# Pieces of weights by GpSimd only behind z's normalising, and the eighth pair's bias written by ScalarE instead of added by TensorE

## The chip, the cores and the metric

One core of one Trainium2 chip. The time is device microseconds from the first to the last instruction of one execution, the median of several runs. Before the change it is 291.32 us, the median of 3 runs between 291.29 and 292.5.

## What is computed

A transformer block in float32 on 8 batches of 256 tokens with 128 features: `x + layernorm(attention(layernorm(x)))`, then `x + layernorm(ffn(layernorm(x)))`. Cut to what matters:

```python
# attention: 16 heads of 8, relative bias
qkv = x @ W_qkv + b_qkv
scores = einsum('bihd,bjhd->bhij', q, k) / sqrt(8)
rel = clip(i - j + 128, 0, 256)
scores = scores + rel_bias[rel].transpose        # (16, 256, 256), the same for each batch
out = softmax(scores) @ v, then @ W_out + b_out
# feed-forward: ternary weights, 128 -> 512 -> 512 -> 512 -> 128
h = silu((x @ w1) * s1) * ((x @ w2) * s2)
h = gelu((h @ h1) * h1s)
h = gelu((h @ h2) * h2s)
y = (h @ w3) * w3s
```

## The kernel before, in words

Each engine's program is written out by hand and they meet at semaphores alone, so the order within each engine is the order of the source.

**Attention.** The heads are taken as 8 pairs, s = 0 to 7, in each of the batches b = 0 to 7. A pair's scores (two heads, 256 x 256, 1024 columns of PSUM) are computed twice. First for the row maxima of the next batch: TensorE `max_scores` (L1236) and `max_bias` (L1244, the bias table's high part by an identity), then VectorE `maxima` (L685). The maxima are transposed (L1253), kept by ScalarE (`minus_max`, L993) and sent by DMA as an additional row of q. Then for the batch itself: the bias is put into the place first, the products `scores` (L1270) are added, ScalarE takes the exponential into a ring (`probabilities`, L1008), and TensorE forms the weighted sums of v for two pairs together (`weighted`, L1296). There are three places in PSUM for all of this; maxima and scores of a pair take turns in them (`wait_max_place`, `wait_score_place`).

The bias comes in three ways. ScalarE copies it from the table `raw` into the place (`write_bias`, L1015) for pairs 0, 1, 3, 4 and 6; VectorE does for pairs 2 and 5 (L692; 1, 2, 4, 5 and 6 in the last batch). For pair 7 (`BY_PE`) TensorE adds it behind the scores with four products by an identity, of the table's high and low parts (`score_bias`, L1281).

While batch b's scores run, batch b - 1 is finished: its heads are brought back (L1307), weighed by VectorE, transposed, projected (L1320), normalised and added to x (`attn_moments`, `residual`: y), and normalised again to z (`second_norm`, L620), which TensorE transposes (`norm_T`, L1327). A normalising needs a reciprocal root, which GpSimd computes (`inv_std`, L517). Batch b - 1's roots are waited for on GpSimd ahead of the pieces of weights.

**Pieces of weights.** GpSimd splits the 11 pieces of the feed-forward weights into high and low parts during attention (`split_weights`, L559 to L571: a cast, a subtraction, a comparison, a product), as many per batch as `SPLIT_AT` says: none, 1, 1, 2, 3, 3, 1, none. It does so right behind the roots of batch b - 1. At the start GpSimd makes the table's high parts (`table_high`, L525) and pair 7's low part (L540).

**The start.** The first two units of x (two tiles each) are normalised, transposed (`x_T`, L1169) and copied by ScalarE (L940). The first batch's rows of q and k are products of the first unit (`row_products`, L1195), less their low part (`row_lows`, L1202), which ScalarE takes and keeps in turn (L959, L967).

**Feed-forward.** Four chunks of 512 tokens, layer by layer and interleaved, each product with the high and the low part of its input (L1441, L1442). The last batch's attention is finished among them (`heads_T`, `project`), with VectorE's `layer_low` (L818) between its steps.

Of the kernel before, what the change touches and what calls it, by code (L numbers as in the profile page):

```python
# [14 lines left out]
P = 128  # L15
# [42 lines left out]
BY_PE = (7,)  # L58
BY_DVE = (2, 5)
LAST_BY_DVE = (1, 2, 4, 5, 6)  # L60
LOW_AT_SLOT = {2 * s + k: 2 * i + k for i, s in enumerate(BY_PE) for k in range(2)}
# [25 lines left out]
def build(nc, x, wq, wk, wv, bqk, brows, bv, wo, bo, ext, w1, s1, w2, s2, h1, h1s, h2, h2s, w3, w3s,  # L87
          ident_in, out):
    ctx = ExitStack()
    with ctx:  # L90
# [3 lines left out]
        def sem(name):  # L94
            return ctx.enter_context(nc.semaphore(name))
# [44 lines left out]
        rows_at = lo_at + 2 * len(BY_PE) * WIN  # L140
        room = sb("room", [P, max(rows_at + 4 * PAIRS * S, 2 * NK * CH * SLOTS)], F32R)
        table_hi = room[:, hi_at:lo_at].rearrange("p (h c) -> p h c", h=H)
        table_lo = room[:, lo_at:rows_at].rearrange("p (h c) -> p h c", h=2 * len(BY_PE))
# [97 lines left out]
        table_lo_set = sem("table_lo_set")  # L241
# [100 lines left out]
        def by_dve(b):  # L342
            return BY_DVE if b + 1 < B else LAST_BY_DVE

        def by_act(b):
            return tuple(s for s in range(PAIRS) if s not in BY_PE + by_dve(b))

# [158 lines left out]
        def _(pool):  # L506
# [13 lines left out]
            def x_inv_std(u):  # L520
                inv_std(u + 1, UNITS[u][1], UNITS[u][0])
# [10 lines left out]
            x_inv_std(1)  # L532
            x_inv_std(2)
            for s in range(PAIRS):
                table_high(s)
                if s == 5:
                    x_inv_std(3)
            for i, s in enumerate(BY_PE):
                pool.wait_ge(table_hi_pool, s + 1)
                nc.gpsimd.tensor_tensor(table_lo[:, 2 * i:2 * i + 2, :], raw[:, 2 * s:2 * s + 2, :],  # L540
                                        table_hi[:, 2 * s:2 * s + 2, :].bitcast(F32),
                                        ALU.subtract).then_inc(table_lo_set, 1)

            x_inv_std(4)
# [29 lines left out]
            for b in range(B):  # L574
                if b > 0:
                    inv_std((b - 1) * 2 + NU + 1, TPB)
                    inv_std((b - 1) * 2 + NU + 2, TPB)
                for piece in SPLIT_AT[b]:
                    split_weights(piece)
# [23 lines left out]
        def _(dve):  # L603
# [19 lines left out]
            def x_moments(u):  # L623
                first, tiles = UNITS[u]
                dve.wait_ge(x_in[u], 16)
                moments(lambda t: xs[:, first + t, :], tiles, u * 2, first)
# [34 lines left out]
            x_moments(1)  # L661
# [3 lines left out]
            spread_weights(nc.vector.tensor_copy, 0, (0,))  # L665
            dve.wait_ge(brows_in, 16)
# [6 lines left out]
            x_normalize(1)  # L673
            dve.wait_ge(ident_loaded, 16)
            nc.vector.tensor_scalar(minus_ident[:, :], ident[:, :], -1.0, None, ALU.mult).then_inc(minus_set, 1)
            dve.wait_ge(qk_w_in[2], 16)
# [184 lines left out]
            layer_low(0, 0)  # L861
            attn_moments(B - 1)
            layer_low(1, 0, (0, 1))
# [292 lines left out]
        def _(pe):  # L1156
# [49 lines left out]
            row_products(0)  # L1206
            x_T(1)
            pe.wait_ge(minus_set, 1)
            row_products(1)
            row_lows(0)  # L1210
# [46 lines left out]
            def scores(b, s):  # L1257

                if s % RPAIRS == 0:
                    pe.wait_ge(mrow_in[s // RPAIRS], (b + 1) * MROW_DMAS * 16)  # L1260
                tile = score_tile(b * PAIRS + s)
                if s in BY_PE:
                    wait_score_place(pe, b * PAIRS + s)
                elif s in by_dve(b):
                    pe.wait_ge(bias_set_dve, biases_by(by_dve, b, s))
                else:
                    pe.wait_ge(bias_set, biases_by(by_act, b, s))
                for j in range(2):
                    for half in range(2):
                        last = mm(tile[:, half, j * S:(j + 1) * S],  # L1270
                                  rows(k_rows, b, half, s)[:, j * P:(j + 1) * P], rows(q_rows, b, half, s),
                                  start=(s in BY_PE and j == 0), stop=False, skip_group_check=True)
                if s not in BY_PE:
                    last.then_inc(st_ready, 1)

            def score_bias(b, s):
                if b == 0:
                    pe.wait_ge(table_lo_set, BY_PE.index(s) + 1)
                for half in range(2):
                    for part in (table_hi[:, 2 * s + half, :], table_lo[:, LOW_AT_SLOT[2 * s + half], :]):  # L1280
                        last = mm(score_tile(b * PAIRS + s)[:, half, :], identr[:, :], windows(part, 0, P, 2, S),  # L1281
                                  start=False, stop=True, skip_group_check=True)
                last.then_inc(st_ready, 1)
# [70 lines left out]
            for b in range(B):  # L1354
                more = b + 1 < B
                for s in range(PAIRS):
                    if more or s not in BY_PE:
                        scores(b, s)
# [13 lines left out]
                    if s in BY_PE and more:  # L1372
                        score_bias(b, s)
                    if s + 1 in BY_PE and not more:

                        scores(b, s + 1)
                        score_bias(b, s + 1)
# [164 lines left out]
            def ffn(exact):  # L1542
# [20 lines left out]
                whole(layer1, 1, exact, (0, 1))  # L1563
                project(B - 1)
                whole(layer1, 1, exact, (2, 3))
# [88 lines left out]
```

## Time and profile before

| | |
|---|---|
| median of 3 runs | 291.32 us |
| the profiled execution | 292.18 us |
| its span, first to last instruction | 290.38 us |
| TensorE busy | 268.5 us (92%) |
| VectorE busy | 219.3 us (76%) |
| ScalarE busy | 205.9 us (71%) |
| GpSimd busy | 102.4 us (35%) |
| mean granted TensorE clock | 0.99 |

The span is the profiled execution's first to last instruction; the execution's own time has a little around it. Busy shares are averages over stages: attention runs to about 194 us, the feed-forward part from there to the end. A timeline row has the start in us from the span's start, the duration, the engine (PE is TensorE, DVE VectorE, ACT ScalarE, POOL GpSimd), the line, the operation, what it writes and reads, how many instructions of the kind follow each other, and in brackets how long the engine had stood idle and for whom.

### The profile page before, as it was taken

Reading aid. Unit: us, or ns where it says so; the run is one execution under the profiler, and the core shown is the slowest. Engines: PE = TensorE matmul, PEld = TensorE weight load, DVE = VectorE, ACT = ScalarE, POOL = GpSimd, SP = SyncE. Lnnn points to the kernel's source line nnn. Section 1 sums busy time; section 2 is a strip of 40 time slices with the busy share of each in tenths; the row PEclk is TensorE's granted clock in tenths of the full one; section 3 lists DMA queues with packets and bytes.
Section 4 is the critical chain, followed back from the end, with each engine's and each line's share of the span. In section 5 each row is a group of like instructions: output and inputs, shape, how many; then the busy total and the mean of one; then the engine's idle time right before and its main releaser. Section 6 shows DMA issues by size and latency. Waiting matters only on the chain.

```text
span 290.4 us, 5171 instructions
## 1 busy us (share of the span) xinstructions
PE 268.5 (92%) x1875; PEld 180.4 (62%) x1875; DVE 219.3 (76%) x442; ACT 205.9 (71%) x316; POOL 102.4 (35%) x107
## 2 busy tenths in 40 slices
PE   7999989899999999999998998899999999999980
PEld 7756645555555554565554554567887888888860
DVE  3489977889789889889889899848556843673674
ACT  2777777776786786885886876777469976896750
POOL 7616000103504305906966957018630202400111
PEclk9999999999999999999999999999999999999996
DMA  6979506232221263470320200000000000010012
GB/s 166 320 238 142 184 11 208 89 83 77 74 76 38 77 207 124 138 224 8 104 81 19 61 1 3 1 3 1 0 2 0 0 0 2 0 36 2 2 36 77
DMA packets 21356, 21.17 MB, mean 73 GB/s; under 512 B 3664, under 2 KB 18768, under 8 KB 21072
## 3 DMA queue, kind: packets, MB, share of 16 engines
q1 hardware_dynamic: 20464, 20.53, 24.8%
q8 instruction: 17, 0.28, 0.4%
q10 hardware_dynamic: 864, 0.27, 0.4%
q14 instruction: 11, 0.09, 0.1%
HBM read 14.90 MB, written 5.64 MB: 71 GB/s over the span
## 4 chain that ended last, share of the span: by engine, by line
PE 60%; DVE 22%; ACT 9%; issue 5%; DMA 1%; POOL 0%; SPq 0%; ACTq 0%; DVEq 0%
PE place L1441 10%; PE place L1442 10%; PE place L1244 8%; DVE mx L685 7%; PE pv L1296 6%; PE place L1236 4%; ACT ring L1008 4%; DVE y_and_z L620 4%; PE place L1270 4%; DVE stats L609 2%; PE place L1195 2%; DVE place L692 2%; ACT place L1015 2%; PE pv L1442 2%; PE pv L1441 2%
## 5 line engine op out<-in xcount | busy, mean ns | idle before, releaser
L685 DVE TENSOR_REDUCE mx<-place 128x4 f32<-128x1024 f32 x64 | 78.1, 1222 | 13.1 <-PE place L1244 11.8
L517 POOL TENSOR_TENSOR rstd<-mv,mhalf 128x2 f32<-128x2 f32 (+1 forms) x26 | 21.0, 809 | 153.0 <-DVE mv L617 153.0
L1008 ACT ACTIVATE ring<-place 128x1024 f32<-128x1024 f32 x64 | 65.6, 1027 | 6.3 <-PE place L1281 3.0
L1244 PE MATMUL place<-room,identr 128*128 128x512 f32 x128 | 46.9, 447 | 0.0
L1015 ACT COPY place<-raw 128x1024 f32<-128x1024 f32 x37 | 37.7, 1022 | 12.2 <-DVE mx L685 11.9
L1441 PE MATMUL place<-room,w_hi 128*128 128x512 f32 (+1 forms) x116 | 44.6, 387 | 0.7 <-DVE room L818 0.7
L1442 PE MATMUL place<-room,w_hi 128*128 128x512 f32 (+1 forms) x116 | 44.0, 382 | 0.0
L818 DVE TENSOR_TENSOR room<-ring,room 128x512 fp32r<-128x512 f32 x32 | 21.4, 690 | 18.5 <-ACT room L1096 18.5
L1296 PE MATMUL pv<-ring,vx 128*9 128x256 f32 x512 | 33.6, 380 | 0.0
L1270 PE MATMUL place<-room 33*128 33x256 f32 x256 | 31.7, 328 | 1.1 <-DVE place L692 1.0
L1236 PE MATMUL place<-room 33*128 33x256 f32 x256 | 28.3, 297 | 2.9 <-ACT ring L1008 2.7
L1270 PEld LDWEIGHTS place<-room 33*128 33x128 f32 x256 | 18.9, 184 | 15.4 <-issue 12.2
L1020 ACT COPY oT<-pv 128x256 f32<-128x256 f32 x32 | 11.8, 370 | 22.2 <-PE pv L1296 22.1
L1236 PEld LDWEIGHTS place<-room 33*128 33x128 f32 x256 | 19.8, 185 | 10.1 <-issue 6.8
L1441 PEld LDWEIGHTS place<-room,w_hi 128*128 128x128 f32 x116 | 21.8, 188 | 5.1 <-DVE room L818 0.9
L1244 PEld LDWEIGHTS place<-room,identr 128*128 128x128 f32 x128 | 19.0, 188 | 8.6
L1442 PEld LDWEIGHTS place<-room,w_hi 128*128 128x128 f32 x116 | 21.8, 188 | 4.1
L692 DVE COPY place<-raw 128x1024 f32<-128x1024 f32 x19 | 23.2, 1225 | 0.6
L1094 ACT ACTIVATE ring<-place,hs 128x512 f32<-128x512 f32 x27 | 18.5, 686 | 5.9 <-PE place L1442 5.9
L1296 PEld LDWEIGHTS pv<-ring,vx 128*9 128x9 f32 x512 | 10.9, 90 | 17.3 <-issue 9.9
L830 DVE SCALAR_TENSOR_TENSOR ring<-place,hs,raw 128x512 f32<-128x512 f32 x16 | 12.0, 750 | 12.0 <-ACT raw L1073 11.8
L1096 ACT CAST room<-ring 128x512 fp32r<-128x512 f32 x32 | 19.9, 621 | 1.0
(141 smaller groups left out, 442.9 us busy)
## 6 DMA issues: line engine op xcount, KB each, us to landing
raw<-ext SPq DMA_DIRECT2D x8, 384.0 KB, 6.9
room<-q_parts SPq DMA_DIRECT2D x48, 64.0 KB
room<-k_parts SPq DMA_DIRECT2D x48, 64.0 KB
w_lo<-h SPq DMA_DIRECT2D x2, 1024.0 KB, 5.2
q_parts<-w_hi SPq DMA_DIRECT2D x4, 256.0 KB, 3.0
k_parts<-w_hi SPq DMA_DIRECT2D x2, 512.0 KB, 3.4
xs<-x SPq DMA_DIRECT2D x3, 256.0 KB, 5.7
w_lo<-w SPq DMA_DIRECT2D x3, 256.0 KB, 2.7
```

What stands on the lines that cost most here:

```text
L517: nc.gpsimd.tensor_tensor(rstd[:, at:at + width], mv[:, at:at + width, 1], mhalf[:, 0:width], ALU.pow).then_inc(rstd_set, 1)
L685: nc.vector.tensor_reduce(mx[:, s // RPAIRS, :, :, s % RPAIRS].rearrange("p i k -> p k i"), max_tile(b * PAIRS + s)[:, :, :].rearrange("p ...
L692: nc.vector.tensor_copy(score_tile(i)[:, :, :].rearrange("p k (j n) -> p k j n", j=2), pair_windows(raw[:, :, :], i % PAIRS)).then_inc(bia ...
L818: nc.vector.tensor_tensor(lo, act_f[:, half[c], k, :], hi.bitcast(F32), ALU.subtract).then_inc((a1_lo_set, a2_lo_set)[i], 1)
L1008: nc.scalar.activation(probs[:, s % PRING, :, :, :].rearrange("p k j n -> p (k j n)"), score_tile(b * PAIRS + s)[:, :, :].rearrange("p k n ...
L1015: nc.scalar.copy(score_tile(i)[:, :, :].rearrange("p k (j n) -> p k j n", j=2), pair_windows(raw[:, :, :], i % PAIRS)).then_inc(bias_set, 1)
L1236: mm(max_tile(b * PAIRS + s)[:, half, it * S:(it + 1) * S], rows(q_rows, b, half, s)[:, it * P:(it + 1) * P], rows(k_rows, b, half, s), st ...
L1244: last = mm(max_tile(b * PAIRS + s)[:, half, :], identr[:, :], windows(table_hi[:, 2 * s + half, :], 0, P, 2, S), start=False, stop=True, ...
L1270: last = mm(tile[:, half, j * S:(j + 1) * S], rows(k_rows, b, half, s)[:, j * P:(j + 1) * P], rows(q_rows, b, half, s), start=(s in BY_PE ...
L1296: last = mm(pv[32 * r:32 * r + VC, 0:S], vx[:, b * TPB + j, 4 * g + r, :], probs[:, (2 * g + r // 2) % PRING, r % 2, j, :], start=(j == 0) ...
L1441: mm(o, w, hi, start=first, stop=False)
L1442: done = mm(o, w, lo, start=False, stop=last and exact)
```

## The change

1. `BY_PE` goes. Pair 7's bias is written by ScalarE, like that of the other pairs: `by_act` now holds 7 in each batch, `scores` waits for it like the others, `score_bias` and the low table with its GpSimd subtraction are gone. In the last batch, where pair 7's scores stand right behind pair 6's, they stay there.
2. GpSimd waits for `z_set` of the batch, behind its two roots, before it takes pieces of weights.
3. GpSimd makes tables 0 and 1 ahead of the third unit's root, and 6 and 7 behind the fourth unit's normalising (`xn_set` 4).
4. At the start VectorE normalises the first unit and spreads the q weights before the second unit's moments, and negates the identity before the second unit's normalising. TensorE takes the first two row products and the first low product before the second unit's transposes.
5. In the feed-forward part `project` of the last batch comes one output group of layer 1 later, and VectorE takes one low part before `attn_moments` and one behind it.

```diff
-BY_PE = (7,)
...
         def by_act(b):
-            return tuple(s for s in range(PAIRS) if s not in BY_PE + by_dve(b))
+            return tuple(s for s in range(PAIRS) if s not in by_dve(b))
...
             spread_weights(nc.gpsimd.tensor_copy, 1)
             x_inv_std(1)
+            table_high(0)
+            table_high(1)
             x_inv_std(2)
-            for s in range(PAIRS):
+            for s in range(2, 6):
                 table_high(s)
-                if s == 5:
-                    x_inv_std(3)
-            for i, s in enumerate(BY_PE):
-                pool.wait_ge(table_hi_pool, s + 1)
-                nc.gpsimd.tensor_tensor(table_lo[:, 2 * i:2 * i + 2, :], raw[:, 2 * s:2 * s + 2, :],
-                                        table_hi[:, 2 * s:2 * s + 2, :].bitcast(F32),
-                                        ALU.subtract).then_inc(table_lo_set, 1)
-
+            x_inv_std(3)
+
+            pool.wait_ge(xn_set, 4)
+            table_high(6)
+            table_high(7)
             x_inv_std(4)
...
                 if b > 0:
                     inv_std((b - 1) * 2 + NU + 1, TPB)
                     inv_std((b - 1) * 2 + NU + 2, TPB)
+
+                    pool.wait_ge(z_set, b)
                 for piece in SPLIT_AT[b]:
                     split_weights(piece)
...
-            x_moments(1)
             x_normalize(0)
             dve.wait_ge(row_zeros, 1)
             dve.wait_ge(bq_scaled, 1)
             spread_weights(nc.vector.tensor_copy, 0, (0,))
+            x_moments(1)
...
             layer_low(0, 0)
+            layer_low(1, 0, (0,))
             attn_moments(B - 1)
-            layer_low(1, 0, (0, 1))
+            layer_low(1, 0, (1,))
             residual(B - 1)
...
             pe.wait_ge(xT_set, 1)
             row_products(0)
+            row_products(1)
+            pe.wait_ge(minus_set, 1)
+            row_lows(0)
             x_T(1)
-            pe.wait_ge(minus_set, 1)
-            row_products(1)
-            row_lows(0)
...
-                if s in BY_PE:
-                    wait_score_place(pe, b * PAIRS + s)
-                elif s in by_dve(b):
+                if s in by_dve(b):
                     pe.wait_ge(bias_set_dve, biases_by(by_dve, b, s))
                 else:
                     pe.wait_ge(bias_set, biases_by(by_act, b, s))
...
-            def score_bias(b, s):
-                if b == 0:
-                    pe.wait_ge(table_lo_set, BY_PE.index(s) + 1)
-                for half in range(2):
-                    for part in (table_hi[:, 2 * s + half, :], table_lo[:, LOW_AT_SLOT[2 * s + half], :]):
-                        last = mm(score_tile(b * PAIRS + s)[:, half, :], identr[:, :], windows(part, 0, P, 2, S),
-                                  start=False, stop=True, skip_group_check=True)
                 last.then_inc(st_ready, 1)
...
-                whole(layer1, 1, exact, (0, 1))
+                whole(layer1, 1, exact, (0, 1, 2))
                 project(B - 1)
-                whole(layer1, 1, exact, (2, 3))
+                layer1(1, 3, exact)
```

How it moves the instructions. ScalarE's program from pair 5's exponential to the next batch's first bias, in batch b = 1; `ring<-place` are exponentials, `place<-raw` bias copies, `mrow` the maxima kept, `oT` a weighted sum kept. Before:

```order
L1008 ACTIVATE ring<-place 128x1024 [waits pv_ready,st_ready]
L993 CAST mrow<-misc 8x256 [waits mrow_in0,mT_ready]
L1008 ACTIVATE ring<-place 128x1024 [waits pv_ready,st_ready]
L1020 COPY oT<-pv 128x256 [waits pv_ready]
L940 COPY xT<-misc 128x512 [waits v_ready,xnT_ready]
L1015 COPY place<-raw 128x1024 [waits ms_read]
L1008 ACTIVATE ring<-place 128x1024 [waits pv_ready,st_ready]
```

Now:

```order
L1006 ACTIVATE ring<-place 128x1024 [waits pv_ready,st_ready]
L991 CAST mrow<-misc 8x256 [waits mrow_in0,mT_ready]
L1013 COPY place<-raw 128x1024 [waits ms_read]
L1006 ACTIVATE ring<-place 128x1024 [waits pv_ready,st_ready]
L1018 COPY oT<-pv 128x256 [waits pv_ready]
L938 COPY xT<-misc 128x512 [waits v_ready,xnT_ready]
L1013 COPY place<-raw 128x1024 [waits ms_read]
L1006 ACTIVATE ring<-place 128x1024 [waits pv_ready,st_ready]
```

The new copy, pair 7's, stands ahead of pair 6's exponential and waits for the maxima of the pair before the last.

TensorE's program at pair 7 of the same batch: scores (128x256 into a place), maxima of the next batch (128x256, then 128x512 with the identity), z's transposes. Before:

```order
L1270 MATMUL place<-room 128x256 [waits ms_read]
L1270 MATMUL place<-room 128x256 x3
L1236 MATMUL place<-room 128x256 [waits exp_done]
L1236 MATMUL place<-room 128x256 x3
L1244 MATMUL place<-room,identr 128x512 x2
L1281 MATMUL place<-room,identr 128x512 x4
L1327 MATMUL misc<-ident,y_and_z 128x128 [waits z_set,xT_set]
```

Now:

```order
L1266 MATMUL place<-room 128x256 [waits bias_set]
L1266 MATMUL place<-room 128x256 x3
L1234 MATMUL place<-room 128x256 [waits exp_done]
L1234 MATMUL place<-room 128x256 x3
L1242 MATMUL place<-room,identr 128x512 x2
L1313 MATMUL misc<-ident,y_and_z 128x128 [waits z_set,xT_set]
```

The four bias products are gone, and pair 7's scores wait for ScalarE's copy instead of the place alone.

## Rows read from the trace of the kernel before

**Rows 1.** busy time by stretches, one attention batch: PE, PEld, DVE, ACT, POOL

```profile
105.20:126.30 21.10, 20.22 (x172) 11.51 (x172) 18.76 (x33) 15.62 (x24) 10.73 (x10) 1.00 0.40 128
```

**Rows 2.** timeline of ScalarE at the joint from b = 5 to 6

```profile
152.31 1.01 ACT L1008 ACTIVATE ring<-place 128x1024 f32<-128x1024 f32 x1
...
155.90 1.02 ACT L1015 COPY place<-raw 128x1024 f32<-128x1024 f32 x1 [1.09 <-DVE mx L685]
156.85 1.02 ACT L1008 ACTIVATE ring<-place 128x1024 f32<-128x1024 f32 x1
```

**Rows 3.** timeline of VectorE at the same joint

```profile
151.54 1.22 DVE L685 TENSOR_REDUCE mx<-place 128x4 f32<-128x1024 f32 x1
152.68 0.60 DVE L620 TENSOR_SCALAR y_and_z<-y_and_z,mv,rstd 128x128 f32<-128x128 f32 x2
...
154.65 1.22 DVE L685 TENSOR_REDUCE mx<-place 128x4 f32<-128x1024 f32 x1
155.78 1.74 DVE L620 TENSOR_SCALAR y_and_z<-xs,mv,rstd 128x128 f32<-128x128 f32 x2
```

**Rows 4.** timeline of TensorE at the same joint

```profile
154.64 0.40 PE L1236 MATMUL place<-room 33*128 33x256 f32 x4
...
155.53 1.09 PE L1281 MATMUL place<-room,identr 128*128 128x512 f32 x4
157.68 0.41 PE L1327 MATMUL misc<-ident,y_and_z 128*128 128x128 f32 x2 [1.06 <-DVE y_and_z L620]
...
158.36 0.40 PE L1236 MATMUL place<-room 33*128 33x256 f32 x4
```

**Rows 5.** timeline of GpSimd from this joint to the next

```profile
155.48 0.61 POOL L559 CAST w_hi<-w_lo 128x512 fp32r<-128x512 f32 x1
156.18 1.27 POOL L561 TENSOR_TENSOR w_lo<-w_lo,w_hi 128x512 f32<-128x512 f32 x1
...
171.93 0.73 POOL L517 TENSOR_TENSOR rstd<-mv,mhalf 128x2 f32<-128x2 f32 x1 [1.77 <-DVE mv L617]
```

**Rows 6.** groups by line and form: z's normalising (busy us, mean ns)

```profile
L620 DVE TENSOR_SCALAR y_and_z<-xs,mv,rstd 128x128 f32<-128x128 f32 x20 | 12.0, 646 | 0.8 <-POOL rstd L517 0.8
```

**Rows 7.** timeline of ScalarE, pair 7's exponential, b = 0 and 4

```profile
52.95 1.02 ACT L1008 ACTIVATE ring<-place 128x1024 f32<-128x1024 f32 x1 [0.95 <-PE place L1281]
...
136.86 1.03 ACT L1008 ACTIVATE ring<-place 128x1024 f32<-128x1024 f32 x1 [0.93 <-PE place L1281]
```

**Rows 8.** timelines of ScalarE and TensorE in the last batch

```profile
189.00 1.94 ACT L1008 ACTIVATE ring<-place 128x1024 f32<-128x1024 f32 x2 [1.57 <-PE place L1270]
...
190.73 1.05 PE L1296 MATMUL pv<-ring,vx 128*9 128x256 f32 x16
```

**Rows 9.** timelines of VectorE, TensorE and GpSimd at the start

```profile
6.57 0.60 DVE L620 TENSOR_SCALAR xn<-xs,mv,rstd 128x128 f32<-128x128 f32 x2
...
7.31 0.41 PE L1169 MATMUL misc<-ident,xn 128*128 128x128 f32 x2 [0.80 <-DVE xn L620]
...
10.51 0.49 PE L1202 MATMUL place<-z_parts,minus_ident 128*128 128x512 f32 x1
...
5.21 1.20 POOL L382 COPY w_lo<-wk_sb 128x256 f32<-128x256 f32 x2
```

**Rows 10.** timelines of VectorE and TensorE at the tables' high parts

```profile
23.73 3.75 DVE L620 TENSOR_SCALAR xn<-xs,mv,rstd 128x128 f32<-128x128 f32 x4
27.39 2.34 DVE L685 TENSOR_REDUCE mx<-place 128x4 f32<-128x1024 f32 x2
...
28.75 0.50 PE L1236 MATMUL place<-room 33*128 33x256 f32 x4
```

**Rows 11.** timeline of TensorE in the feed-forward part

```profile
220.12 0.71 PE L1320 MATMUL misc<-wo_sb,onT 128*128 128x128 f32 x4 [0.69 <-ACT onT L1024]
```

**Rows 12.** busy time by stretches at the end; PEclk is the granted clock

```profile
282.90:285.20 2.30, 0.00 (x0) 0.00 (x0) 2.16 (x13) 0.00 (x0) 1.08 (x2) 1.00 0.38 117
285.20:290.40 5.20, 0.00 (x0) 0.00 (x0) 1.69 (x5) 0.00 (x0) 0.32 (x1) 0.50 0.19 55
```

More of the change, by code:

```diff
@@ L55 @@
 SLOT_HEAD = [s + HALF * k for s in range(PAIRS) for k in range(2)]
-BY_PE = (7,)
 BY_DVE = (2, 5)
 LAST_BY_DVE = (1, 2, 4, 5, 6)
-LOW_AT_SLOT = {2 * s + k: 2 * i + k for i, s in enumerate(BY_PE) for k in range(2)}
 def windows(ap, start, step, count, width):
@@ L139, in build @@
         hi_at, lo_at = 0, H * WIN
-        rows_at = lo_at + 2 * len(BY_PE) * WIN
+        rows_at = lo_at
         room = sb("room", [P, max(rows_at + 4 * PAIRS * S, 2 * NK * CH * SLOTS)], F32R)
         table_hi = room[:, hi_at:lo_at].rearrange("p (h c) -> p h c", h=H)
-        table_lo = room[:, lo_at:rows_at].rearrange("p (h c) -> p h c", h=2 * len(BY_PE))
         q_rows = room[:, rows_at:rows_at + 2 * PAIRS * S].rearrange("p (a h n) -> p a h n", a=2, h=PAIRS)
@@ L240, in build @@
         table_hi_pool = sem("table_hi_pool")
-        table_lo_set = sem("table_lo_set")
         dve_order = sem("dve_order")
@@ L672, in _ @@
                                     ALU.mult).then_inc(low_bias_set, 1)
-            x_normalize(1)
             dve.wait_ge(ident_loaded, 16)
             nc.vector.tensor_scalar(minus_ident[:, :], ident[:, :], -1.0, None, ALU.mult).then_inc(minus_set, 1)
+            x_normalize(1)
             dve.wait_ge(qk_w_in[2], 16)
@@ L1271, in scores @@
                                   rows(k_rows, b, half, s)[:, j * P:(j + 1) * P], rows(q_rows, b, half, s),
-                                  start=(s in BY_PE and j == 0), stop=False, skip_group_check=True)
-                if s not in BY_PE:
-                    last.then_inc(st_ready, 1)
-            def score_bias(b, s):
-                if b == 0:
-                    pe.wait_ge(table_lo_set, BY_PE.index(s) + 1)
-                for half in range(2):
-                    for part in (table_hi[:, 2 * s + half, :], table_lo[:, LOW_AT_SLOT[2 * s + half], :]):
-                        last = mm(score_tile(b * PAIRS + s)[:, half, :], identr[:, :], windows(part, 0, P, 2, S),
-                                  start=False, stop=True, skip_group_check=True)
+                                  start=False, stop=(j == 1), skip_group_check=True)
                 last.then_inc(st_ready, 1)
@@ L1356, in _ @@
                 for s in range(PAIRS):
-                    if more or s not in BY_PE:
+                    if more or s < PAIRS - 1:
                         scores(b, s)
@@ L1371, in _ @@
                         max_bias(b + 1, s)
-                    if s in BY_PE and more:
-                        score_bias(b, s)
-                    if s + 1 in BY_PE and not more:
+                    if s + 2 == PAIRS and not more:
                         scores(b, s + 1)
-                        score_bias(b, s + 1)
                     if s == 0:
```

## The prediction

> **What bounds the kernel now.** I read the busy time by stretches, then the four engines' timelines at the place where one batch's attention passes into the next, then the start and the last batch. In an attention batch TensorE is busy 20.22 of 21.10 us, VectorE 18.76 and ScalarE 15.62 [rows 1]. So TensorE sets the pace, with under 1 us of slack per batch, and a product taken out is worth its own time only until another chain ends last. I follow the joint between the batches b = 5 and 6 (s is the pair, 0 to 7).
>
> ScalarE takes pair 6's exponential at 152.31, writes pair 0's bias of the next batch at 155.90 and takes pair 7's exponential at 156.85 [rows 2]. VectorE's maxima that free pair 7's score place end at 151.54 + 1.22 = 152.76, the next maxima at 155.87, and z's normalising begins at 155.78 [rows 3]. TensorE forms the maxima of pair 7 at 154.64, the four bias products of pair 7 (L1281) from 155.53 to 156.62, waits 1.06 for z, transposes it at 157.68 and reaches the next batch's maxima at 158.36 [rows 4].
>
> **GpSimd's wait for z.** The two instructions that normalise z take 1.74 at this joint. The same form needs 0.60 on y, where GpSimd is idle [rows 3]. Beside z run GpSimd's first cast of a weight piece, 155.48 to 156.09, and its subtraction, 156.18 to 157.45 [rows 5]; z's second half ends at 157.52, just behind the subtraction. Over the whole trace z's form takes 12.0 us for 20 instructions [rows 6], where ten pairs at 0.60 would make 6.0: 6 us more, of which five joints (b = 2 to 6) hold 1.1 each. With the wait z takes 0.60 there. The bounds for one joint are 0 (where the time is hidden) and 1.14.
>
> GpSimd's own work then starts when z ends, about 156.4 instead of 155.48. Behind it on GpSimd's queue stand the pieces and then the next batch's two reciprocal roots. After the three pieces of this batch it has 1.77 us of idle before the next root [rows 5]; 0.9 of later start and a batch shorter by 0.5 leave some 0.4. So I cost this at nothing, and name it as a danger: without that cover VectorE's normalising of y waits for the root.
>
> **Pair 7's bias from TensorE to ScalarE.** TensorE loses 32 products, 4 in each batch, 1.09 by the row [rows 4]. ScalarE gains 8 copies of 1.02 that hold it 0.95 (155.90 to 156.85) [rows 2]. The copy is issued ahead of pair 6's exponential. It can start when the maxima end, at 152.8, so that exponential moves from 152.31 to 153.75 and ends at 154.76. Its first customer is TensorE's maxima of pair 7, now at 154.64: they slip 0.2, to 154.8. The 1.4 us of delay are nearly all hidden in a stretch in which ScalarE was idle.
>
> Now the joint with both edits. TensorE is through pair 7's maxima about 0.9 after 154.8 (154.64 to 155.53 before), at 155.7. z is ready at 155.78 + 0.60 = 156.4 and transposed at 156.5, not 157.68. The next batch's pair 0 needs its bias, which waits for VectorE's maxima (155.87): 155.90 + 1.02 = 156.92, scores at about 157.0. The next batch's first maxima need pair 7's exponential, 156.85 + 1.02 = 157.87, and start at 157.9 instead of 158.36 [rows 2, 4]. **This joint gains 0.45**, not 1.1 and not 2.1: maxima, copy and exponential on VectorE and ScalarE are late next. The other joints, by the same steps:
>
> - b = 0: pair 7's exponential waits 0.95 for L1281 [rows 7], but the copy pushes pair 6's exponential and with it pair 7's maxima by 0.5; gain 0.4.
> - b = 1, 2, 3 and 5: 0.5 each, 2.0 together.
> - b = 4: TensorE has one more group of products between pairs 5 and 6, so the delayed exponential is hidden; pair 7's own exponential, held by L1281 for 0.93 [rows 7], moves by all of it, and z with it: 1.2.
> - b = 6: next comes VectorE's bias for the last batch, not maxima. It follows z directly and moves with it: 1.1.
>
> Together 4.7. **The last batch gives some back.** There pair 7's scores stand ahead of the weighted sum of pairs 4 and 5 on TensorE. ScalarE takes pairs 5's and 6's exponentials back to back from 189.00 [rows 8]. The copy goes between them, 189.95 to 190.97; scores (0.43) and blank products (0.33) follow, and the weighted sum starts at 191.8 instead of 190.73 [rows 8]. L1281's removal here only turns work into waiting. Loss 1.1; bounds 0.5 and 1.7, since I don't know which of the gains before it reach this point in full.
>
> **The start.** The first unit's normalising moves ahead of the second unit's moments, from 6.57 to about 5.3. TensorE's transposes at 7.31 had waited 0.80 for it, so at most 0.8 is to be had [rows 9]. But it now runs beside GpSimd's spreading of the k weights, 5.21 to 6.41 [rows 9], as z did beside the pieces, so I take 0.4. Against it, the second unit's transposes now come behind the first low product (10.51) on TensorE [rows 9], and ScalarE, which copies that unit before it takes the next rows, gets to them later by 0.4 to 0.8. Net 0, bounds 0.5 either way.
>
> The Trainium skill ("SBUF — State Buffer", section "Who interferes with whom") says that the pair goes whole to whichever instruction of the two engines started first, and the other fully blocks until it ends. By that rule the first unit's normalising would stand still at both of GpSimd's spreading copies, and the start would lose a few tenths instead of nothing. The trace agrees at z; for the start no run here shows it yet.
>
> **The tables' high parts** 0 and 1 go ahead of a root on GpSimd, 6 and 7 behind the fourth unit's normalising, which takes 3.75 beside them [rows 10] and would take some 1.1. VectorE gains 2.6, but the first maxima that waited for it end at about 28.6, and TensorE's maxima of pair 6 start at 28.75 behind other work [rows 10]: gain 0.1, bounds 0 and 0.6. Leaving out the low table costs nothing. **The feed-forward part**: TensorE waits 0.69 once for the last batch's head copy ahead of the projection [rows 11]; the projection moves one output group later, so most of this goes: 0.5, bounds 0 and 0.7. VectorE's low parts move with it and are not late.
>
> **The sum**: 4.7 - 1.1 + 0 + 0.1 + 0.5 = 4.2. I take off 0.5, because the joints were worked one at a time and a shorter batch brings the next root and row loads nearer: 3.7. The profiled execution took 292.18 (span 290.38), so 288.5. It lay 0.86 above the median of 291.32, so **287.6** for the median.
>
> **Rivals.**
> 1. *The joints pay less* (0.14). Only z's wait pays, where TensorE visibly waits for z (1.06 here, about as much in b = 6), and the copy on ScalarE eats what L1281 gave. For it: in four joints the sum above lets through only 0.5 of 2.1. Gain 1.7: 289.6.
> 2. *TensorE's time comes back whole* (0.06): 8 x 0.95 = 7.6, if the chain of maxima, copy and exponential has more slack than its rows show: 283.7. Against it: 155.87, 156.85, 157.87 has no gap.
> 3. *The clock falls in the last batch* (0.10). TensorE would stand about 2 us there, waiting for the copied bias. At the kernel's end the granted clock is at half (0.50, the lower level of 1.2 GHz) from 285.2 on, after 2.3 us without a product, and at full in those 2.3 [rows 12]. If it falls, the first 12 products of the feed-forward part and the last weighted sums take twice their 3 us or so: 3 lost, 290.6. The Trainium skill ("TensorE: Matmul & The Clock Gate", section "What's actually happening") has an idle TensorE put back to the lower level; this trace bears that out only for the end.
> 4. *Slower* (0.05): pair 6's exponential is paid for. It decides where its delay of 1.4 exceeds what stands between it and pair 7's maxima (1.2 now). If those maxima come nearer, each batch pays 1.4 and gets 0.95 back, with z's gain hidden behind it: 8 x 0.49 = 3.9 lost, 295.2. Against it: at this joint the slip is 0.2.
> 5. *The wait doesn't bite* (0.03), because GpSimd is late by itself and z has passed, and copy and L1281 cancel: 291.3.
>
> **How the numbers follow.** Forecast 0.62. A measurement of this kernel can tell 0.5% (1.46 us) from no change, so faster means below 289.86: forecast 0.61, rival 1 0.11, rival 2 0.06 and 0.03 of rival 3, together 0.81. Within: 0.13. Slower: 0.06. The bounds of the terms are about 2 either way; with rival 1 and half of rival 3 the range is 285.6 to 290.5.
>
> **What would show it.** z's pair at 0.60 in all batches, with GpSimd's cast behind it. A copy from raw ahead of pair 6's exponential, TensorE waiting some 0.2 before pair 7's maxima and 0.5 to 0.8 before z's transposes. Joints 0.5 shorter, the one of b = 4 1.2. TensorE idle about 2 us before the last scores, at full clock. The first maxima at the old time. I'm wrong if VectorE's normalising of y waits for the root in b = 6, if ScalarE has no idle time left at the joint, or if the granted clock shows half near 190.

## The result, and the profile after

The changed kernel takes 300.06 us, the median of four executions (299.17 to 301.21), against 291.65 for the kernel before in the same comparison: a ratio of 1.028, 95% interval 1.026 to 1.031. The change makes the kernel 8.4 us slower. The forecast was 287.6 us. Executions that stand well apart from the others of a version are left out of the ratios and their intervals; the medians below are over all of them.

The page of the changed kernel's profile, its span and the granted clock in 40 slices:

```profile
span 297.2 us, 5117 instructions
...
PEclk9999999999999999999995699958999999999996
```

Before, the only low digit was the last. Now there are two more low spots inside the attention part. Busy time by stretches places them (behind the length stand TensorE, its weight loads, VectorE, ScalarE and GpSimd; the last columns are the granted clock, the DMA share and GB/s):

```profile
151.00:155.00 4.00, 3.29 (x32) 1.64 (x24) 3.90 (x10) 3.13 (x5) 1.66 (x3) 1.00 0.07 19
155.45:169.10 13.65, 13.57 (x76) 7.39 (x76) 6.33 (x9) 7.27 (x11) 12.46 (x11) 0.50 0.11 32
169.10:187.00 17.90, 15.87 (x146) 8.77 (x144) 15.17 (x29) 14.03 (x20) 6.09 (x6) 1.00 0.01 2
187.00:193.00 6.00, 4.12 (x42) 2.28 (x38) 5.18 (x14) 3.91 (x6) 0.73 (x1) 1.00 0.00 0
193.00:203.24 10.24, 9.08 (x50) 5.10 (x51) 2.15 (x9) 4.87 (x8) 0.70 (x1) 0.50 0.01 2
```

TensorE runs 13.65 us at 0.50, the lower level of 1.2 GHz, behind the joint from b = 5 to 6, and 10.24 us in the last batch. It is busy 13.57 and 9.08 us of them, and VectorE, which was busy 18.76 of 21.10 [rows 1], only 6.33 of 13.65: TensorE is the bound there.

Until the first fall, the joint is the one that was forecast. TensorE:

```profile
151.78 0.50 PE L1266 MATMUL place<-room 33*128 33x256 f32 x4
152.33 0.50 PE L1234 MATMUL place<-room 33*128 33x256 f32 x4
152.76 0.74 PE L1242 MATMUL place<-room,identr 128*128 128x512 f32 x2
154.04 0.41 PE L1313 MATMUL misc<-ident,y_and_z 128*128 128x128 f32 x2 [0.54 <-DVE y_and_z L617]
154.57 0.50 PE L1266 MATMUL place<-room 33*128 33x256 f32 x4
155.53 0.79 PE L1234 MATMUL place<-room 33*128 33x256 f32 x4 [0.45 <-ACT ring L1006]
156.25 1.22 PE L1242 MATMUL place<-room,identr 128*128 128x512 f32 x2
```

The bias products of [rows 4] are gone, z's transposes wait 0.54 instead of 1.06 and come at 154.04 instead of 157.68. The next batch's first maxima start at 155.53 instead of 158.36, 2.83 us ahead. They are also where the clock has fallen: 0.79 for the four where such a group takes 0.40 to 0.50, and L1242's pair right behind 1.22 against 0.74 above. ScalarE at the joint:

```profile
150.31 1.02 ACT L1013 COPY place<-raw 128x1024 f32<-128x1024 f32 x1 [0.40 <-DVE mx L682]
151.26 1.02 ACT L1006 ACTIVATE ring<-place 128x1024 f32<-128x1024 f32 x1
...
153.41 1.02 ACT L1013 COPY place<-raw 128x1024 f32<-128x1024 f32 x1 [0.87 <-DVE mx L682]
154.36 1.02 ACT L1006 ACTIVATE ring<-place 128x1024 f32<-128x1024 f32 x1
```

VectorE, and GpSimd, at the same joint:

```profile
153.29 0.60 DVE L617 TENSOR_SCALAR y_and_z<-xs,mv,rstd 128x128 f32<-128x128 f32 x2
```

```profile
152.33 0.70 POOL L513 TENSOR_TENSOR rstd<-mv,mhalf 128x2 f32<-128x2 f32 x1 [2.38 <-DVE mv L614]
153.96 0.61 POOL L554 CAST w_hi<-w_lo 128x512 fp32r<-128x512 f32 x1 [0.93 <-DVE y_and_z L617]
```

Pair 7's bias is copied ahead of pair 6's exponential; z takes 0.60, not the 1.74 of [rows 3], and the cast stands behind it. The roots still find GpSimd idle (2.38). The last batch, TensorE and then ScalarE:

```profile
191.13 0.74 PE L1266 MATMUL place<-room 33*128 33x256 f32 x8
193.67 0.80 PE L1266 MATMUL place<-room 33*128 33x256 f32 x4 [1.79 <-ACT place L1013]
194.40 0.79 PE L1160 MATMUL pv<-blank 128*128 128x256 f32 x2
195.12 1.90 PE L1282 MATMUL pv<-ring,vx 128*9 128x256 f32 x16
```

```profile
191.68 1.02 ACT L1006 ACTIVATE ring<-place 128x1024 f32<-128x1024 f32 x1 [1.57 <-PE place L1266]
192.60 1.02 ACT L1013 COPY place<-raw 128x1024 f32<-128x1024 f32 x1
```

TensorE waits 1.79 us for the copy, with the weighted sum of pairs 4 and 5 behind it. The clock falls in this wait, at 193.0, and sixteen products then take 1.90 where they took 1.05 [rows 8].

### The profile page after: what moved, and what is told of

It reads as the page before. It is cut to its first block, busy times and chain, and to the rows that moved or that the text cites. A ratio compares the mean times of both kernels' runs of the same rounds, so it can differ in the third digit from the quotient of the medians.

```text
span 297.2 us, 5117 instructions
## 1 busy us (share of the span) xinstructions
PE 272.6 (92%) x1843; PEld 179.8 (60%) x1843; DVE 212.2 (71%) x442; ACT 213.6 (72%) x324; POOL 100.6 (34%) x106
## 4 chain that ended last, share of the span: by engine, by line
PE 66%; DVE 17%; ACT 10%; issue 5%; DMA 1%; POOL 1%; ACTq 0%; POOLq 0%; DVEq 0%
PE place L1424 11%; PE place L1425 10%; PE place L1242 9%; PE pv L1282 8%; DVE mx L682 7%; PE place L1234 5%; ACT ring L1006 4%; PE place L1266 4%; DVE place L689 3%; PE misc L1293 3%; ACT place L1013 2%; PE place L1193 2%; PE misc L1172 2%; PE pv L1425 2%; PE pv L1424 2%
## 5 line engine op out<-in xcount | busy, mean ns | idle before, releaser
L1013 ACT COPY place<-raw 128x1024 f32<-128x1024 f32 x45 | 45.9, 1023 | 15.7 <-DVE mx L682 15.7
L1242 PE MATMUL place<-room,identr 128*128 128x512 f32 x128 | 48.4, 460 | 0.0
L1282 PE MATMUL pv<-ring,vx 128*9 128x256 f32 x512 | 37.0, 411 | 0.5 <-ACT ring L1006 0.5
L1266 PE MATMUL place<-room 33*128 33x256 f32 x256 | 33.1, 339 | 3.5 <-ACT place L1013 2.0
L1234 PE MATMUL place<-room 33*128 33x256 f32 x256 | 29.5, 308 | 4.1 <-ACT ring L1006 3.9
L1266 PEld LDWEIGHTS place<-room 33*128 33x128 f32 x256 | 19.9, 192 | 18.8 <-issue 12.3
L1234 PEld LDWEIGHTS place<-room 33*128 33x128 f32 x256 | 20.7, 193 | 11.8 <-issue 8.8
L1242 PEld LDWEIGHTS place<-room,identr 128*128 128x128 f32 x128 | 19.6, 193 | 8.9 <-issue 0.9
```

The costliest lines, as they stand in the source:

```text
L1013: nc.scalar.copy(score_tile(i)[:, :, :].rearrange("p k (j n) -> p k j n", j=2), pair_windows(raw[:, :, :], i % PAIRS)).then_inc(bias_set, 1)
L1234: mm(max_tile(b * PAIRS + s)[:, half, it * S:(it + 1) * S], rows(q_rows, b, half, s)[:, it * P:(it + 1) * P], rows(k_rows, b, half, s), st ...
L1242: last = mm(max_tile(b * PAIRS + s)[:, half, :], identr[:, :], windows(table_hi[:, 2 * s + half, :], 0, P, 2, S), start=False, stop=True, ...
L1266: last = mm(tile[:, half, j * S:(j + 1) * S], rows(k_rows, b, half, s)[:, j * P:(j + 1) * P], rows(q_rows, b, half, s), start=False, stop= ...
L1282: last = mm(pv[32 * r:32 * r + VC, 0:S], vx[:, b * TPB + j, 4 * g + r, :], probs[:, (2 * g + r // 2) % PRING, r % 2, j, :], start=(j == 0) ...
```

## The experiments

Two theories had to be told apart first. **The clock theory**: nothing on the chains of waits costs time; TensorE, with 1.09 us less work per batch at the joint and a wait in the last batch, has its clock lowered, and that is the loss. **Its rivals**: the shorter z alone does it; or the copies on ScalarE cost the time and the clock only goes along.

### The parts of the change by themselves

*GpSimd's wait alone*, in the kernel before:

```
                     inv_std((b - 1) * 2 + NU + 2, TPB)
+
+                    pool.wait_ge(z_set, b)
```

> The kernel before with only GpSimd's wait for z ahead of its pieces of weights. Theory (the clock falls because TensorE lost pair 7's bias products): TensorE still adds that bias at every joint, the granted clock stays full from 6 to 285 us and the time is 1.5 to 2 us below before, 289.5 to 290. Rival A (the shorter joint alone drops the clock, or the weights that come later are paid for): half clock near 155 us for some 10 us or more, and 293 to 297. Rival B (the wait changes nothing): 291.3 within 0.3.

Measured: 291.54 us (290.44 to 292.26 over ten executions) against 291.73, ratio 0.999 (0.998 to 1.000). The clock is full up to the end, so rival A is out; but the gain is 0.2 us, hardly clear of none, and not 1.5 to 2. TensorE at the joint b = 5 to 6:

```profile
156.28 1.09 PE L1283 MATMUL place<-room,identr 128*128 128x512 f32 x4
157.26 0.41 PE L1329 MATMUL misc<-ident,y_and_z 128*128 128x128 f32 x2
```

The wait for z is gone; TensorE's own chain now ends last, with the bias products in it.

*Pair 7's bias alone*, in the kernel before:

```
-BY_PE = (7,)
...
-                    if s in BY_PE and more:
-                        score_bias(b, s)
-                    if s + 1 in BY_PE and not more:
+                    if s + 2 == PAIRS and not more:
                         scores(b, s + 1)
-                        score_bias(b, s + 1)
```

> The kernel before with only pair 7's bias moved from TensorE to ScalarE, in all batches. Theory: TensorE has 1.05 us less work per batch and waits some 2 us ahead of the last scores; the clock falls there (near 190 to 195 us) for about 10 us, which costs 4 to 5 us of the 10, so 294 to 296, and it may fall at a joint too (then 298 to 301). Rival A (the shorter z alone drops it): no half clock before 285 us, 290.9 to 292.4. Rival C (no clock, the copies on ScalarE cost the time): over 296 with the clock full.

Measured: 299.17 us (297.56 to 306.55, four executions), 7.4 above the kernel before; the ratio of those that lie together is 1.021 (1.019 to 1.023). The page's clock row has both falls, one at the joint behind b = 6 this time (176 to 187 us), one in the last batch (193 to 204):

```profile
PEclk9999999999999999999999985958999999999996
```

TensorE waited 1.67 for z at the joint from b = 5 to 6, with no product in the place of L1281, and 1.67 again at the next joint, where the clock fell in the wait, at 176.2:

```profile
176.86 0.66 PE L1306 MATMUL misc<-ident,y_and_z 128*128 128x128 f32 x2 [1.67 <-DVE y_and_z L611]
```

*All but the bias*, and *all but GpSimd's wait* (the changed kernel with that part taken back):

> The changed kernel with pair 7's bias left on TensorE as before (its low parts of the table too). Theory: no half clock before the last few us; joints 0.35 us shorter each, the other parts a few tenths, so 288.7 to 289.8. Rival A: half clock at a joint, 293 or more.

> The changed kernel with GpSimd casting its pieces beside z's normalising as before. Theory: the last batch is the changed kernel's, so the clock falls near 193 us for about 10 us; at the joints TensorE waits longer than in the changed kernel and has no bias products, so a fall at one of them too is more likely than not: 295 to 301. Rival A (only the shorter z drops it): no half clock before 285, 290.5 to 291.5.

Measured: 290.78 us without the bias part (290.18 to 291.17, ratio 0.996, 0.995 to 0.997), clock full up to the last slice; 302.54 without the wait (300.47 to 308.44, ratio 1.034, 1.028 to 1.041). Its profile has the clock low in five stretches, but it is of the 308.44 execution; the other three had mean clocks of 0.936 to 0.952, the changed kernel 0.945 to 0.951. So the bias part brings the falls. That GpSimd's wait makes them fewer isn't shown by these two. The first of the two lies 1 us above its forecast range: the joints pay less than forecast as long as TensorE has the bias products.

### Less work on TensorE, nothing on ScalarE

The clock theory's sharpest case: in the kernel before, three of the four bias products are left out in the batches 0 to 6, with no copy in their place.

```
+                parts = [(table_hi[...], table_lo[...]) for half in range(2)]
+                if b + 1 < B:
+                    parts = [(), parts[1][0:1]]
                 for half in range(2):
-                    for part in (table_hi[...], table_lo[...]):
+                    for part in parts[half]:
```

> The kernel before with three of the four products of pair 7's bias left out in batches 0 to 6 (that pair's bias is incomplete there; the last batch has it whole), and no copy on ScalarE in their place. It takes 0.75 us of TensorE's work out of each joint and moves nothing else. Theory (the clock falls for TensorE's missing work): half clock behind one joint or more, and 293 to 300. Rival (it falls for what ScalarE's copies change): full clock, 291.0 to 291.8, or a few tenths less.

Measured: 291.22, 296.33, 296.97 and 297.72 us; the mean granted clock was 0.987 in the first and 0.959 to 0.961 in the others. The kernel before, in 17 executions of the same comparison, stayed between 290.98 and 292.67. Over all the comparisons of this section, 55 executions of kernels that keep the four bias products (the kernel before, GpSimd's wait alone, all but the bias) all had a mean clock of 0.988 or more. The profile (TensorE, then stretches):

```profile
153.16 0.40 PE L1284 MATMUL place<-room,identr 128*128 128x512 f32 x1
155.30 0.66 PE L1330 MATMUL misc<-ident,y_and_z 128*128 128x128 f32 x2 [1.74 <-DVE y_and_z L620]
155.89 0.80 PE L1270 MATMUL place<-room 33*128 33x256 f32 x4
```

```profile
151.00:155.00 4.00, 2.56 (x28) 1.30 (x27) 3.90 (x9) 1.83 (x3) 2.46 (x3) 1.00 0.01 3
155.00:168.60 13.60, 13.30 (x74) 7.15 (x74) 7.08 (x9) 7.17 (x11) 12.08 (x11) 0.50 0.15 41
```

Taking work out of TensorE, and nothing else, made the kernel some 5 us slower in three executions of four: 13.6 us at half clock behind the same joint as in the changed kernel, and in this profile 3.4 more from 182.3. ScalarE's copies aren't needed for it.

### The work given back as zero products

The changed kernel, with products on a tile of zeros that nobody reads (the kernel has such a stream already, L1160). *Six at each joint, for b = 1 to 6:*

```
                             pe.wait_ge(mrow_set, b * RANGES + 3)
+                        stream(misc, blank, blank, 6)
                         norm_T(b - 1)
```

> The changed kernel with six products on the zero tile (nobody reads them) ahead of z's transposes at each of the joints b=1 to 6, where pair 7's bias products stood; they read and write nothing that another engine makes just then. Theory (TensorE's missing work at the joint lets the clock fall): no half clock from 6 to 190 us, the one in the last batch stays (10 us at half, some 5 us lost): 293 to 296. Rival (the falls have nothing to do with TensorE's own work there, e.g. they follow the wait for the exponential's place): half clock at a joint as often as in the changed kernel, 299 to 301.

*Fourteen in the last batch's wait:*

```
                     if s + 2 == PAIRS and not more:
+                        pe.wait_ge(oT_set, b * GROUPS + 2)
+                        stream(pv, blank, blank, 14)
                         scores(b, s + 1)
```

> The changed kernel with fourteen products on the zero tile in the last batch's wait for pair 7's bias, and none at the joints. Theory: no fall near 193 us; the joint's fall (13.65 us at half in the changed kernel's profile) stays, 293 to 297. Rival: the fall near 193 stays, 299 to 301.

*Both:*

> Both sets of zero products in the changed kernel. Theory: full clock from 6 to 285 us and the joints' gain left over (z's transposes of the joint behind batch 5 were 3.6 us earlier than before when the clock fell; the zero products may take 0.2 to 0.3 us of each joint, and the last batch's wait some 2 us): 287 to 289.5, below the kernel before. Rival (the clock was not the loss, or the joint's gain is not kept): 291 or more.

Measured: 292.56 us at the joints alone (three executions 292.3 to 292.6, ratio 1.002, 0.999 to 1.004; one 299.91 with the clock at 0.951 against 0.978); 296.74 in the last batch alone (ratio 1.017, 1.014 to 1.019); 290.34 with both (ratio 0.994, 0.991 to 0.998). The clock rows of the three, in this order:

```profile
PEclk9999999999999999999999999959999999999995
```

```profile
PEclk9999999999999999999995559999999999999995
```

```profile
PEclk9999999999999999999999999999999999999995
```

In these profiles each set of zero products takes away the fall at its own place and leaves the other. With both, 9.7 us of the changed kernel's 300.06 are back, for products that compute nothing; 290.34 is still 0.8 above the range expected of this version, and the 292.56 lies 0.4 below its own. The last batch also settles whether the zero products work only by moving what follows. TensorE with the joints' products alone, then with both sets:

```profile
186.02 0.74 PE L1266 MATMUL place<-room 33*128 33x256 f32 x8
188.56 0.59 PE L1266 MATMUL place<-room 33*128 33x256 f32 x4 [1.80 <-ACT place L1013]
```

```profile
186.65 1.93 PE L1160 MATMUL pv<-blank 128*128 128x256 f32 x14
188.52 0.50 PE L1266 MATMUL place<-room 33*128 33x256 f32 x4
```

The scores behind the wait start at the same time, 188.56 and 188.52, and only the first of the two falls to half clock, at 188.9. The rival, that the falls don't hang on TensorE's own work, is out.

### The last batch in another order

*The weighted sum of pairs 4 and 5 ahead of pair 7's scores*, no zero products:

```
-                    if s + 2 == PAIRS and not more:
-                        scores(b, s + 1)
                     if s == 0:
...
                         if s % 2 == 0:
                             weighted(b, s // 2 - 1)
+                    if s + 2 == PAIRS and not more:
+                        scores(b, s + 1)
```

> The changed kernel with the last batch's weighted sum of pairs 4 and 5 issued ahead of pair 7's scores, so that TensorE doesn't wait 1.8 us for ScalarE's copy with that sum behind it; no zero products are added. Theory: the fall near 193 us goes or comes much more seldom, and the wait's 1.1 to 1.8 us are won besides; the joint's fall stays: 292 to 296. Rival (the last fall comes from something else in that stretch): half clock near 193 as before, 298 to 300.

Measured: 289.07 us at a mean clock of 0.985 (the profiled one, with half clock at a joint for only 3.4 us), and 294.05, 295.33, 295.69 at 0.950 to 0.964. The profile has no fall in the last batch:

```profile
PEclk9999999999999999999998999999999999999996
```

Of the other three only the mean clock is known: it says that they fell for longer, not where. Since the executions scatter so, no ratio is given for this version or for the one with the products left out.

### Both repairs, and the price of each

> The changed kernel with both repairs: six zero products ahead of z's transposes at each joint, and in the last batch the weighted sum of pairs 4 and 5 ahead of pair 7's scores. Theory: full clock from 6 to some 280 us; against the version with zero products in both places (290.3) the last batch's 1.8 us wait is gone too, so 288 to 289.5. Rival (a clock near its edge falls in some executions all the same): a median over 291, with single times near 288.

> The same with ten zero products at each joint in place of six (some 1.1 us of TensorE, as much as the bias products had). Theory: TensorE is not the bound at the joint (it waits there for ScalarE's exponential), so the four products more cost 0 to 0.3 us at each of six joints: 0 to 1.8 us above the version with six, and the clock is at least as safe. Rival: as the bias products' time is back whole, the joint's gain is gone: 291 to 292.

> The version with ten zero products and the last batch's new order, with GpSimd casting its pieces beside z's normalising as before. It prices GpSimd's wait where the bias is ScalarE's. Theory (the two edits need each other: the wait alone gave 0.2 us since TensorE's bias products ended last at the joint anyway; with those on ScalarE z ends last): 2 us or more above the version with the wait if the clock holds, and more if it falls. Rival (the wait is worth 0.2 us here too): within 0.5 us of it.

Measured: **289.18 us** for the new order with six zero products (288.54 to 290.39, ratio 0.992, 0.989 to 0.994), the fastest version, 2.9 us below the kernel before and 10.9 below the changed one. Its span and clock row:

```profile
span 286.8 us, 5183 instructions
...
PEclk9999999999999999999999999999999999999996
```

The profile is one of three executions at 288.5 to 288.6 with a mean clock of 0.991 to 0.992; the other three took 289.8 to 290.4 at 0.983 to 0.987, so a short fall in them can't be ruled out.

With ten at each joint it is 290.12 (twelve executions, 289.00 to 291.93, ratio 0.995, 0.993 to 0.997), 0.94 above. In the profiles, both at full clock, the four more products are dearer: z's transposes at the joint b = 5 to 6 lie 111.68 us behind the first batch's weighted sum (44.95 to 156.63) with ten, 109.76 with six and 113.03 before. That is 0.4 us per joint for four, and more than half of the joints' gain is gone. Without GpSimd's wait it is 296.71 (293.23 to 299.32, ratio 1.012), with three falls of 3 to 7 us in the profile of its slowest execution; "2 us or more above, and more if the clock falls" holds, but since it fell, the wait's price at full clock can't be read from the time.

## Why the prediction was wrong, point by point

I compare distances on TensorE from batch 0's weighted sum at 44.65 (44.99 in the changed kernel, 45.37 with GpSimd's wait alone, 45.57 with the bias alone, 45.08 in the fastest version), since that point scatters by itself from one execution to the next.

**The joints b = 0 to 4 were right.** z's transposes of successive batches lie 21.59, 21.08, 21.01 and 20.60 us apart before (first at 73.40, last 157.68) and 21.09, 20.66, 20.27 and 19.51 after (72.51 to 154.04): gains of 0.50, 0.42, 0.74 and 1.09. The forecast for b = 1 to 4 had 0.5, 0.5, 0.5 and 1.2. The 1.23 from the anchor to the first of them hold b = 0 (forecast 0.4) and what z itself gains inside a joint. From the anchor to z at the joint b = 5 to 6 the changed kernel is 3.98 shorter. GpSimd's wait alone gives 1.14 there and the bias alone 1.95, 3.09 in sum: the two edits need each other, since each alone leaves the other's chain last. Of the wait's 1.14 only 0.62 are left at the last z transposes (151.79 from the anchor, 152.41 before), and 0.2 in the medians; where the rest went wasn't followed.

**The joint b = 6 was mis-sized**: forecast 1.1, measured about 0. (The joint b = 5, forecast 0.5, gave 0.2 there with its zero products: z to z 19.99 against 20.21.) In the fastest version z is transposed at 174.83, early, but the next step isn't. ScalarE, VectorE and TensorE there:

```profile
174.19 1.02 ACT L1013 COPY place<-raw 128x1024 f32<-128x1024 f32 x1 [0.87 <-DVE mx L682]
175.14 1.02 ACT L1006 ACTIVATE ring<-place 128x1024 f32<-128x1024 f32 x1
176.06 0.36 ACT L1026 CAST z_parts<-misc 128x256 fp32r<-128x256 f32 x1
```

```profile
176.46 0.42 DVE L740 TENSOR_TENSOR z_parts<-misc,z_parts 128x256 fp32r<-128x256 f32 x1 [0.66 <-ACT z_parts L1026]
176.80 2.34 DVE L689 COPY place<-raw 128x1024 f32<-128x1024 f32 x2
```

```profile
178.07 0.50 PE L1266 MATMUL place<-room 33*128 33x256 f32 x4 [0.40 <-DVE place L689]
```

ScalarE's cast of z stands behind a copy and an exponential on its own queue, VectorE's low part waits 0.66 for it, and the last batch's bias comes behind that. The forecast said VectorE's bias "follows z directly and moves with it"; the row between them is ScalarE's. In sum, up to the last batch's scores the fastest version gained 2.76, and its zero products took some 0.9 (six joints at 0.15, see below): 3.7, where the forecast had 4.7.

**The last batch's loss was right** as a wait: forecast 1.1. From the scores behind the joint b = 6 to the last z transposes it is 16.66 us before (180.40 to 197.06), 17.80 with zero products in both places (177.92 to 195.72) and 16.60 in the new order (178.07 to 194.67). The new order takes back 1.1 to 1.2.

**The feed-forward part was too small**: forecast 0.5, bounds 0 and 0.7; measured 0.95. From the last z transposes to VectorE's last operation it is 89.47 us before (197.06 to 286.53) and 88.52 in the fastest version (194.67 to 283.19). The products around the projection:

```profile
218.46 0.39 PE L1425 MATMUL place<-room,w_hi 128*128 128x512 f32 x1
218.68 0.61 PE L1306 MATMUL misc<-wo_sb,onT 128*128 128x128 f32 x4
219.05 0.48 PE L1424 MATMUL place<-room,w_hi 128*128 128x512 f32 x1
```

From the product ahead of the projection to the one behind it are 0.59 us, not 1.55 (219.04 to 220.59 before). The stall cost more than the 0.69 named in [rows 11], since the products beside it overlap where it is gone.

**Start and tables**: the first unit's normalising starts at 5.34, forecast 5.3, takes 1.22 beside GpSimd and not 0.60, and TensorE's transposes come at 6.71 against 7.31 [rows 9]. The anchor at 45 us lies at 44.86 to 45.09 in the profiles that have the new start, at 44.41, 44.65, 45.37 and 45.57 in those that haven't: against that scatter a gain or loss of the start of some tenths can't be told. The fourth unit's normalising takes 1.12 as forecast, and nothing waited for it [rows 10].

**With the clock held the sum was nearly right.** The fastest version's last VectorE operation, counted from the anchor, is 3.77 us nearer than before: 2.76 up to the last batch's scores, 0.06 in the last batch, 0.95 behind. Forecast 3.7. It has a better last batch (1.1) and pays for zero products (0.15 per joint: 109.76 to z at the joint b = 5 to 6 against 109.02 with the new order alone). For the changed kernel itself at full clock the measured parts would make an estimated 3.7 - 1.1 + 0.95 = 3.5, against the forecast 3.7. That this is so near is in part luck: the joint b = 6 was 1.1 too high, the feed-forward part 0.45 too low, and 0.5 had been taken off for no single cause.

**What failed is the clock**, in two steps.

First, the joints. The text followed who waits for whom and nothing else; no step asked what removing 1.09 us of products does to an engine that already waits 1.06 beside them. The sum of 4.7 holds the clock at full through every joint and gives no reason for it. The bias products had a second use that no dependency shows: they were all that TensorE did between pair 7's maxima and its wait for z, and without them the clock fell at a joint in the changed kernel, with the bias alone and with three of them left out.

Second, the size. Rival 3 named the mechanism for the last batch, and the place was right (193.0). But it had 3 us and a chance of 0.10. Against the version with both sets of zero products, z to z over the first fall is 25.76 us (154.04 to 179.80) and not 19.98 (154.70 to 174.68), and from the scores to the last z 21.81 (183.06 to 204.87) and not 17.80. So the first fall, which the forecast didn't have at all, costs 5.8 us, the second 4.0, some 0.4 us for each microsecond at half clock. 9.8 in all: about 300.06 less the 290.34 of that version. Rival 3's 3 us counted the products right behind the wait; the low clock lasted 10.24 us, with TensorE busy for 9.08 of them.

The Trainium skill ("TensorE: Matmul & The Clock Gate", section "What's actually happening"), which has an idle TensorE put back to the lower level, was cited with the remark that this trace bears it out only for the end. The runs here go further than the page: the clock also fell inside the kernel, for an engine that had never stood idle for long. In the 4 us ahead of the first fall its longest wait is 0.54; the second fall comes 1.1 us into the wait of 1.79.

What stays open is which trait of TensorE's work decides. The length of the wait and the busy time just before don't tell a joint that falls from one that doesn't. The two rows are the changed kernel up to its first fall, and the kernel before at its own joint, where it kept the clock:

```profile
151.45:155.45 4.00, 2.91 (x24) 1.42 (x16) 3.50 (x9) 3.13 (x5) 2.11 (x3) 1.00 0.12 34
154.50:158.50 4.00, 2.94 (x24) 2.06 (x22) 3.97 (x6) 2.65 (x4) 3.51 (x4) 1.00 0.00 1
```

TensorE is busy 2.91 and 2.94 of 4 us, and the longest wait is 0.54 in the one that fell and 1.06 in the one that didn't. With the bias alone the joint b = 5 to 6 had the same 1.67 us wait as the next, where the clock fell, and kept it; the changed kernel's joints up to b = 4 have the same waits of 0.54 or none. The place moves between versions and executions; that falls come at all follows TensorE's work. A version with real work instead of zero products in these places was not tried.

## What to carry to other kernels

Before work is taken off a TensorE that is nearly always busy, look at where it waits beside that work. If a wait stands next to the removed products, the clock may be what pays, even where the wait gets no longer: here 1.09 us less work per batch cost 9.8 us. Then read the granted clock by stretches first and the waits second; if it has fallen, test with products on zeros in the wait. Keep them few: six cost 0.15 us per joint here, ten some 0.5. And two edits on the two chains that meet at one point are worth more together than apart (3.98 against 3.09 here), so pricing them one at a time, or dropping one because it measures nothing alone, misleads.

## What the runs showed of the hardware

- The kernel with less to do was the slower one: leaving out three products per joint, 0.7 us of TensorE's time (1.09 for the four, 0.40 for the one left), cost some 5 us in three executions of four.
- One fall lasts long. In the profiles here half clock lasted from 3.4 us (the new order alone) over 6.8 (joint products alone, 188.9 to 195.7), 10.24 and 13.65 to 20.5 us (155.3 to 175.8 with zero products in the last batch alone), with TensorE busy 89% or more of the four longer ones.
- Busy time and the length of a wait don't foretell it: a stretch with 2.91 of 4 us busy ended in a fall, one with 2.94 and a wait twice as long did not.
- Executions of one program differ in it: the new order alone gave 289.07 at a clock of 0.985 and 295.69 at 0.959. A spread of 2% where the kernel before has 0.6% was the sign of a clock near its edge.
- VectorE's pair of normalising instructions at the start took 1.22 beside GpSimd's copies where it had taken 0.60 behind them [rows 9]. The Trainium skill ("SBUF — State Buffer", section "Who interferes with whom") has the engine that comes second block until the other's instruction ends; the 0.62 more agree with that in kind.
